# Ten propagation hops on TensorE: from straight code to a loop of five passes over two hops

## The reference, cut to what matters

```python
K = 10; ALPHA = 0.1; BETA = 0.9
deg_row = maximum(segment_sum(ones, row), 1.0)
deg_col = maximum(segment_sum(ones, col), 1.0)
w = rsqrt(deg_row[row] * deg_col[col])

def spmm(feat):
    msg = feat[col] * w[:, None]
    return segment_sum(msg, row, num_segments=n)
h = x
out = h
for _ in range(K):
    out = spmm(out) * BETA + h * ALPHA
...
return out / theta
```

## Time and profile before

| | |
|---|---|
| three runs | 2786.09, 2791.23, 2801.3 us |
| profiled execution | 2786.09 us, its span 2784.4 us, 1.7 us outside it |
| TensorE busy with matmuls | 1848.1 us, 66% of the span |
| the ten hops | from 638 to 1157 us of the span |
| VectorE, ScalarE, GpSimd busy | 56%, 31%, 34% of the span |
| granted TensorE clock, mean | 0.735 |

### The profile page before, as it was taken

How to read it: one execution, slowest core, us unless ns; L and a number is a source line. 1 busy time by engine, 2 the same in 40 slices (tenths; PEclk the granted TensorE clock), 3 DMA queues, 4 the chain that set the end, 5 groups by cost and what they waited for, 6 DMA issues and landing times. The chain is left out here.

```text
span 2784.4 us, 49745 instructions
## 1 busy us (share of the span) xinstructions
PE 1848.1 (66%) x14611; PEld 1442.6 (52%) x14611; DVE 1564.6 (56%) x4031; ACT 862.9 (31%) x1484; POOL 946.4 (34%) x1182
## 2 busy tenths in 40 slices
PE   1777777778999999687525555545445555545588
PEld 0333344458999999654414343433334344433477
DVE  7866866765444444555425564555555555555753
ACT  1587566651111111121212222222222222222420
POOL 3311222222000000000066666666666666666100
PEclk9978988988999999898755555555555555555599
DMA  4211111120000000700132222222222222222200
GB/s 138 92 49 43 42 57 70 57 77 2 2 2 1 2 2 25 289 1 4 36 47 50 50 49 49 49 49 48 49 48 50 50 50 49 49 49 48 68 1 19
DMA packets 86643, 133.04 MB, mean 48 GB/s; under 512 B 48616, under 2 KB 55656, under 8 KB 86462
## 3 DMA queue, kind: packets, MB, share of 16 engines
q1 hardware_dynamic: 40398, 83.53, 8.9%
q0 software_dynamic: 25344, 38.98, 7.0%
q10 hardware_dynamic: 20720, 8.06, 1.3%
HBM read 95.89 MB, written 34.58 MB: 47 GB/s over the span
## 5 line engine op out<-in xcount | busy, mean ns | idle before, releaser
L1426 POOL DMA_INDIRECT counts<-p_rows,rows x784 | 746.3, 952 | 496.7 <-issue 224.1
L1655 PE MATMUL ps_e_z<-e_w_q,counts 128*128 128x96 f32 x1568 | 363.9, 427 | 251.7 <-ACT counts L1591 210.6
L927 PE MATMUL ps_hop<-y,counts 128*128 128x192 f16 x6250 | 518.4, 246 | 13.2 <-DVEq L818 13.2
L927 PEld LDWEIGHTS ps_hop<-y,counts 128*128 128x128 f16 x6250 | 516.6, 98 | 14.9 <-issue 13.3
L1655 PEld LDWEIGHTS ps_e_z<-e_w_q,counts 128*128 128x128 f32 x1568 | 341.5, 330 | 287.8 <-ACT counts L1591 242.1
L560 DVE TENSOR_TENSOR hot_w<-iota_w,places_now 128x1600 f16<-128x1600 f16 x300 | 297.2, 991 | 158.1 <-PE ps_counts L586 138.0
L586 PE MATMUL ps_counts<-hot_w,hot_p 128*128 x1196 | 287.9, 373 | 116.8 <-DVE hot_p L560 73.1
L1666 PE MATMUL ps_e_seg<-counts 128*128 128x192 f16 x784 | 141.2, 359 | 309.9 <-DVE counts L1466 148.0
L1666 PEld LDWEIGHTS ps_e_seg<-counts 128*128 128x128 f16 x784 | 100.2, 138 | 393.9 <-DVE counts L1466 210.3
L1591 ACT ACTIVATE counts<-ps_e_u 96x1024 f32<-96x1024 f32 x98 | 100.0, 1020 | 643.5 <-remote 592.4
L527 POOL TENSOR_TENSOR places_now<-places,origins (+1 forms) x302 | 125.3, 416 | 422.5 <-DVE hot_p L560 281.0
(11 more groups left out here) (401 smaller groups left out, 2485.4 us busy)
## 6 DMA issues: line engine op xcount, KB each, us to landing
counts<-count_rows SPq DMA_DIRECT2D x30, 800.0 KB, 6.7
count_rows<-attr_split SPq DMA_DIRECT2D x25, 800.0 KB, 3.8
counts<-p_rows,rows POOLq DMA_INDIRECT x784
e_attr<-attr_parts SPq DMA_DIRECT2D x99, 72.0 KB
attr_parts<-attr_split SPq DMA_DIRECT2D x9, 784.0 KB, 16.0
attr<-attr_parts SPq DMA_DIRECT2D x50, 140.6 KB
e_dst_rows<-dst_row SPq DMA_DIRECT2D x99, 64.0 KB
e_w_q<-q_rows ACTq DMA_DIRECT2D x392, 12.0 KB
```

Source lines behind the costliest of these rows:

```text
L927: mm = pe.matmul(ps[:, r, 0:2 * D], k.counts[:, m, b, :], y[:, hop % 2, b, :], start=b == 0, stop=b == NB - 1)
L1426: nc.gpsimd.indirect_dma_start(z[:, slot, j, :], None, k.p_rows, bass.IndirectOffsetOnAxis(rows, 0)) \
L1655: mm = pe.matmul(ps_z[:, two, j // (STEP_TILES // 2), at:at + D], u_hot[:, two, j * P:(j + 1) * P], w_q[:, fed, j // Q_TILES, :], start=Tr ...
```

## The change

TensorE's part of `propagate` becomes a hardware loop over five pairs of hops. Inside, the two hops of a pair stay written out, so which copy of `y` is read is still a constant. What depends on the number of the hop, the value of every wait, is now worked out from the loop's register. The matmuls, their order and their operands are the same. The other engines' parts are the same.

```diff
-            for hop in range(HOPS):
-                for m in range(NB):
-                    n, r = hop * NB + m, m % RING
-
-                    pe.wait_ge(hop_taken, n * 2 + 2)
-                    for b in range(NB):
-                        if m == 0:
-                            pe.wait_ge(y_ready, hop * NB + (b + 1))
-                        mm = pe.matmul(ps[:, r, 0:2 * D], k.counts[:, m, b, :], y[:, hop % 2, b, :],
-                                       start=b == 0, stop=b == NB - 1)
-                    mm.then_inc(hop_done, 1)
+            with pe.Fori(0, HOPS // 2) as pair:
+                for odd in range(2):
+                    hop = pair * 2 + odd
+                    for m in range(NB):
+                        n, r = hop * NB + m, m % RING
+
+                        pe.wait_ge(hop_taken, n * 2 + 2)
+                        for b in range(NB):
+                            if m == 0:
+                                pe.wait_ge(y_ready, hop * NB + (b + 1))
+                            mm = pe.matmul(ps[:, r, 0:2 * D], k.counts[:, m, b, :], y[:, odd, b, :],
+                                           start=b == 0, stop=b == NB - 1)
+                        mm.then_inc(hop_done, 1)
```

## The result

The changed kernel takes 2811.28 us (median of 6 runs, 2802.81 to 2816.22), the kernel before 2791.4 us on the same chip (6 runs, 2786.09 to 2801.3): a ratio of 1.0068, 95% interval 1.0053 to 1.0085, slower by 0.68%. The prediction was 2808.0 us, range 2796 to 2826. The profiled execution is at 2801.42 us, its span 2799.7 us.

What follows compares the result with a forecast made beforehand. TensorE's gapless matmul stream in the ten hops was taken as the bound. Jumps 12.7, held sequencer 1 and clock 3 us sum to 16.7 us, added to the median 2791.2: 2808 us, range 2796 to 2826.

Steps and rivals of the forecast that it cites:

- The code at the loop's start is gone: At four jumps back in TensorE's loop, code of about ten packets must be fetched anew; jumps that fetch, 0.63.
- 299 jumps of 76 ns: In TensorE's short loop, jumps of 76 ns, the longest 233, cited for the rival of nearly free jumps (0.25 with well covered).
- F = 3.5 us: At each jump back, one code fetch from issue to use: a 2.5 us small transfer plus a packet's 1.0 us.
- the bounds of 1.0 and 6.7 us: Limits of one code fetch at a jump: a packet's own time, and the landing of 800 KB; 3 to 25 us.
- The lead of 1.37 us: At a hop's start TensorE's sequencer runs 1.37 us, some 17 matmuls, ahead of the engine, all that can hide added work.
- The queue of 64 instructions: A lead of 32 matmuls, 2.6 us, hides 5 us of the jumps; 2803 us; nearly free or well covered jumps 0.25.
- 0.113 us a step: In a hop's first block, one ALU_OP and a matmul take the sequencer 0.113 us where the engine needs 0.082.
- Jumps, 12.7 us: Four jumps back to the loop's start, each losing 3.2 us until the weight load of b = 24; 3 to 25 us.
- the 2.16: Time in us from a hop's first matmul until the new `y` lets b = 24 start.
- Held sequencer, 1 us: The unmet wait for `y` block 24 holds the sequencer, then some 0.15 us of register work: 0.1 us per hop.
- Clock, 3 us: After a jump's idle the granted clock falls, up to 1.7 us, counted at every second jump; 0 to 7 us.
- The sign "released by nothing that the profile names": Four gaps of 2 to 3 us in TensorE's stream at even hops' starts, with no releaser named in the trace.

Runs made afterwards that it cites:

- the probe: Straight kernel plus ten three-pass loops over 60 to 1250 small matmuls ahead of the degree sums; taken branches 0.2 us or 3.3 to 4.8 us.
- the repeat: The changed kernel again, with a clamp at zero on two waits of the counting stage: 2804.7 us against 2795.01, ratio 1.0043.

## Why the prediction was right

- **The code at the loop's start is gone: right.** Four long branches, packets at each, and the price disappears where the body fits (0.2 us, nine jumps) and comes back at every jump only from 1800 instructions on. The changed body has over 2500. One reading beside it was wrong: the earlier trace rows does not show 299 jumps of 76 ns, but 200 branches that were not taken and 99 jumps of 0.21 us. The sum had 0.2 us for count and branch, so it does not suffer.
- **F = 3.5 us: right in size, by luck.** The four branches took 3.53 us on average (in all kernels' hops 3.3 to 3.9, up to 4.8 in the probe); the estimate was a small transfer's 2.5 us plus a packet's 1.0. Nothing showed that a fetch of code behaves like that transfer, and the bounds of 1.0 and 6.7 us left 3 to 25 us for the jumps.
- **The lead of 1.37 us: right.** The first branch began 1.36 us ahead of where hop 2 would have begun, and each gap was the branch less 1.08. The other three gaps stand in the same relation to their branches. The queue of 64 instructions that the Trainium skill gives, page "TensorE: Matmul & The Clock Gate", table at its head, would by the prediction's estimate make it 2.6 us; at no jump here was it seen.
- **0.113 us a step: right.** The steps were 0.1125 us but for a few longer ones. It matters behind a jump alone: elsewhere the lead hides it.
- **Jumps, 12.7 us: 13.7 measured.** The two without a fall of the clock cost 3.16 and 3.33 us. The other two, with their own longer branches and the same 0.98 us behind the gap (2.70 + 0.98, 2.54 + 0.98), would be 3.68 and 3.52. The 3.2 us a jump of the prediction came close because its errors partly cancel. The hop began 2.4 us late instead of 2.6, but b = 0 to b = 24 then took 3.0 us instead of 2.7, and the even hops before reached b = 24 after 2.03 us, not the 2.16 that was read at an odd one.
- **Held sequencer, 1 us: nothing.** At the odd hops b = 24 goes after 0.19 us of idle, as before. The sequencer was held as foreseen: the value for the next m is worked out at 691.46, just as that load starts. But it takes 37 ns, not some 150, and the next load goes 82 ns after the one for b = 24, the engine's own pace. This step was wrong, by 1 us.
- **Clock, 3 us: about 2 measured,** 15.8 less 13.7, from falls behind two jumps of four; the fourth jump's longer stall at b = 23 may take 0.2 us of it. In the hops of all kernels it fell behind 6 of 16 long jumps. It did not behind the three in the middle of a hop, too few to say that the place matters.
- **Not foreseen:** the second packet moves only after the jump is over and can come late too. That it stalls the stream where the target lies near the end of its packet is borne out by the stall some 70 instructions behind it in two bodies, and by its absence in a third whose target lies elsewhere; where the packets' borders lie was not read.
- **The sign "released by nothing that the profile names": wrong.** Each gap was put down to the last block of `y`. Only in the middle of a hop did the trace say "issue".

The sum was 16.7 us and the stretch shows 15.8. The medians differ by 19.9 us, in the repeat by 9.7. The two intervals, 15 to 24 us and 8 to 16, both hold 15.8.

## What to carry to other kernels

In this kernel a hardware loop cost nothing by its register values, as long as the sequencer was ahead, and nothing by its jump, as long as its body fitted the code at hand: up to about 1600 instructions (800 matmuls) on TensorE without a miss. From 1800 on each pass paid a fetch of 3.3 to 4.8 us, of which the sequencer's lead, less the register work behind the jump, hid about 1 us. Put the jump where TensorE has no register-paced block behind it. In the trace look at the longest COMPARE_BRANCH, not at the releaser that the gap names, and count the instruction packets in the second pass: none means that the body fits.

## What the runs showed of the hardware

- A taken branch of TensorE cost 0.21 to 0.25 us with its target at hand, near or far (one of over 100 in the probe 0.35); one not taken 67 to 88 ns; one to code that is gone 3.3 to 4.8 us.
- TensorE kept a body of 1730 instructions and lost one of 1800; of two jumps over 1667 one missed.
- Behind a long jump in the hops the second packet starts 3.0 to 3.6 us after the first. The straight hops never waited for a packet: before, 48 came in 510 us without a gap in the stream.
- The same gap does not always cost the clock: behind gaps of 2.3 to 2.9 us in a dense stream it fell from 1.00 to 0.50 in 6 cases and stayed in 10.
